# Attention scores from float32r halves on two 64-row halves of TensorE's array, in place of bf16 thirds on 96 rows

## The chip, the cores and the metric

The kernel runs on one core of one Trainium2 chip, in one launch. The metric is the device time in microseconds (us), the median of three runs: 1236.69 us, with 1232.07 and 1240.46 as the ends.

## What is computed

A transformer layer with float32 inputs and outputs: layer normalisation, causal attention from a latent, residual; layer normalisation, a top-2 mixture of 8 experts, residual. Cut to what matters here:

```python
# x: (4, 1024, 256), 16 heads of 16
c_kv = xn @ W_DKV                      # latent of 64
k = (c_kv @ W_UK).reshape(b, t, h, hd)
v = (c_kv @ W_UV).reshape(b, t, h, hd)
q = (xn @ W_UQ).reshape(b, t, h, hd)
scores = einsum('bqhd,bkhd->bhqk', q, k) / sqrt(hd)
scores = where(causal, scores, -inf)
probs = softmax(scores, axis=-1)
ctx = einsum('bhqk,bkhd->bqhd', probs, v).reshape(b, t, d)
x = x + ctx @ W_O
# then x = x + top-2 mixture of 8 experts of layernorm(x): W1 (256 -> 2 x 512, gated), W2 (512 -> 256)
```

## The kernel before

The program has four stages, one after the other, each ended by all engines: projection, attention, routing and experts.

*Projection* takes 4096 tokens in 8 chunks of 512. TensorE transposes the normalised tokens and makes the latent, q, k and v with float32 matmuls. q and k must keep float32 accuracy in bf16 matmuls, so each is split into three bf16 parts whose sum is the value: ScalarE copies the PSUM result to bf16 (L203), VectorE subtracts that from the PSUM result (`rest`, L266), ScalarE copies the rest to bf16 (L208), and GpSimd subtracts again for the third part (L183). SP then stores the parts of q and k (L144) and v (L147) in HBM.

*Attention* takes 64 pairs of batch and head in 16 quads of four heads. For a quad SP loads stacks `q_st` and `k_st` of 96 rows: six runs of 16 rows, in each one part of q against one part of k (`RUNS`), so that one contraction over 96 rows gives the score. A second set of three rows holds the row maxima, also in three bf16 parts, against rows of ones in `k_st`, so that a contraction over 99 rows gives score minus maximum. Four stacks (`RING`) are in use.

A quad has 12 units, each a block of 128 queries (or keys) by up to 512 columns, for the four heads. There are two passes over the scores. The maximum pass makes scores with queries as rows (`max_scores`, L666) in three PSUM banks (`NM`); VectorE reduces each block to its maximum, with the causal mask on diagonal blocks (L596, L599). After the 12 units VectorE combines the halves and splits the maxima in five small steps (`combine`, L568 to L583), TensorE transposes them (L714), ScalarE copies them to SBUF (L622), and SP copies them into the stack (L515). The probability pass makes scores with keys as rows (`prob_scores`, L684) in three other banks (`NS`), ScalarE takes the exponential (L640), GpSimd clears the triangle of diagonal blocks (L554), and TensorE multiplies with v (`products`, L703), the four heads side by side in strips of 32 columns, plain float32.

The order on TensorE is written out by hand. The probability pass runs 16 units (`LEAD`) behind the maximum pass and the products 2 units (`LAG`) behind the probabilities; within a unit, a maximum matmul and a probability matmul alternate, and the four products' matmuls come behind the four pairs:

```python
for unit in range(TOTAL + LEAD + LAG):
    if turned_at(unit) is not None:
        max_rows_transposed(turned_at(unit))
    for n in range(unit * QUAD, (unit + 1) * QUAD):
        if unit < TOTAL:
            max_scores(n)
        if 0 <= unit - LEAD < TOTAL:
            prob_scores(n - LEAD * QUAD)
    if unit - LEAD - LAG >= 0:
        products(unit - LEAD - LAG)
```

Each matmul waits until its bank is free: `max_scores` for VectorE (`bank_free`), `prob_scores` for ScalarE (`prob_ok`, three blocks back). `prob_scores` of a quad's first block also waits until the maximum rows have landed (`rows_in`). While attention runs, SP loads w1 (8 slices of 1 MB) and `FC_EARLY` = 3 slices of w2 for the experts, one per quad; the fourth slice of w2 is loaded in the routing stage (L917), between the loads of the next batch and the store of x2 (L923). VectorE's residual addition for the next batch (L1031) waits for that store.

*Routing* projects the context, adds the residual, normalises, picks experts and scatters rows by expert, batch by batch. *Experts* runs 71 tiles of 128 rows through W1 and W2 in plain float32 matmuls, one of which is recorded as two instructions.

## Time and profile before

| | |
|---|---|
| median of 3 runs | 1236.69 us (1232.07 to 1240.46) |
| span of the profiled execution | 1240.9 us |
| TensorE busy | 1069.9 us, 86% of the span |
| VectorE | 787.0 us, 63% |
| ScalarE | 491.9 us, 40% |
| GpSimd | 390.4 us, 31% |
| DMA | 121.22 MB, mean 98 GB/s |

The time to compare with is the median; durations of single instructions come from the profiled execution, whose span is given beside it. In the rows below PE is TensorE, PEld its weight loads, DVE VectorE, ACT ScalarE, POOL GpSimd and SP SyncE; L666 is line 666 of the kernel. Times are in us, unless a column says ns.

### The profile page before, as it was taken

To read this page: it belongs to the slowest core of one execution; us is meant where nothing else is said; L and a number is where in the kernel's file an instruction comes from. 1 tells how busy PE (TensorE), PEld (TensorE's weight loads), DVE (VectorE), ACT (ScalarE), POOL (GpSimd) and SP (SyncE) were. 2 spreads that over 40 slices of the span, in tenths; PEclk is the share of its full clock that TensorE was granted. 3 is DMA by queue.
4 is the path that set the end of the run, shared out by engine and by line. 5 is a ranking of instruction groups with operands and counts; after the bars stand their busy time and mean duration, and the time that the engine had idled before them with its cause. 6 is when DMAs were issued, how large, how long until landed. Compare 5 with 4: busy or idle time off the path is not lost. (4 is left out here: it accounts for less than half of the span.)

```text
span 1240.9 us, 19607 instructions
## 1 busy us (share of the span) xinstructions
PE 1069.9 (86%) x5364; PEld 554.3 (45%) x5365; DVE 787.0 (63%) x2352; ACT 491.9 (40%) x1043; POOL 390.4 (31%) x721
## 2 busy tenths in 40 slices
PE   6897599999999999998587553089999999999995
PEld 2443123333333333332176543046666666666663
DVE  5654599999999999894057443245555555555553
ACT  2333047777777777777501212012122122122121
POOL 2224513333333333333403235512222222222222
PEclk9878569999999999999987565589999999999998
DMA  2665974444466644400266641212232232232232
GB/s 91 208 189 188 199 157 104 122 113 113 116 141 135 132 82 79 80 20 30 66 220 193 225 124 68 103 39 44 46 50 42 45 49 42 44 49 42 44 49 25
DMA packets 102396, 121.22 MB, mean 98 GB/s; under 512 B 26352, under 2 KB 81776, under 8 KB 102320
## 3 DMA queue, kind: packets, MB, share of 16 engines
q1 hardware_dynamic: 89024, 102.55, 32.5%
q0 software_dynamic: 13296, 17.77, 8.6%
q8 instruction: 34, 0.56, 0.2%
q14 instruction: 42, 0.34, 0.1%
HBM read 70.27 MB, written 49.63 MB: 97 GB/s over the span
## 5 line engine op out<-in xcount | busy, mean ns | idle before, releaser
L640 ACT ACTIVATE b_prob<-b_prob_ps 128x512 f32<-128x512 f32 (+3 forms) x768 | 318.0, 506 | 103.2 <-PE b_prob_ps L684 101.2
L596 DVE CUSTOM_DVE_ANT_0 b_max_ps<-b_max_ps,b_mask_max 128x384 f32<-128x384 f32 (+3 forms) x512 | 246.7, 503 | 50.4 <-PE b_max_ps L666 47.9
L666 PE MATMUL b_max_ps<-b_k_st,b_q_st 96*128 96x512 bf16 (+3 forms) x768 | 253.5, 345 | 24.2 <-DMA b_k_st<-k_parts 21.8
L684 PE MATMUL b_prob_ps<-b_q_st,b_k_st 99*128 99x512 bf16 (+3 forms) x768 | 239.5, 330 | 10.5 <-ACT b_prob L640 6.6
L554 POOL TENSOR_SCALAR_AFFINE_SELECT b_prob<-b_prob 128x128 f32<-128x128 f32 x512 | 146.6, 292 | 308.6 <-ACT b_prob L640 300.9
L1352 POOL DMA_INDIRECT out_dram<-e_y,e_token x71 | 110.1, 1551 | 326.1 <-DVE e_y L1406 310.4
L599 DVE TENSOR_REDUCE b_neg_max<-b_max_ps 128x1 f32<-128x512 f32 x256 | 176.1, 688 | 5.1 <-PE b_max_ps L666 2.6
L666 PEld LDWEIGHTS b_max_ps<-b_k_st,b_q_st 96*128 96x128 bf16 x768 | 74.4, 99 | 202.0 <-DVE b_neg_max L596 110.1
L703 PE MATMUL b_acc_ps<-b_prob,b_v_aug 128*32 128x512 f32 (+3 forms) x1536 | 163.4, 498 | 0.2 <-POOL b_prob L554 0.2
L1459 PE MATMUL e_g_ps<-w_sb,e_rowsT 128*128 x284 | 135.5, 600 | 0.3 <-issue 0.3
L1459 PE MATMUL e_a_ps<-w_sb,e_rowsT 128*128 x284 | 134.0, 594 | 0.0
L684 PEld LDWEIGHTS b_prob_ps<-b_q_st,b_k_st 99*128 99x128 bf16 x768 | 74.1, 98 | 92.9 <-ACT b_prob L640 60.7
L1424 ACT ACTIVATE e_gate<-e_g_sum 128x512 f32<-128x512 f32 x71 | 44.7, 629 | 164.1 <-DVE e_g_sum L1386 164.1
L1429 ACT ACTIVATE e_hiddenT<-e_hiddenT_ps 128x512 f32<-128x512 f32 x71 | 42.4, 597 | 168.2 <-PE e_hiddenT_ps L1467 168.2
L1476 PE MATMUL e_y_ps<-w_sb,e_hiddenT 128*128 x426 | 103.7, 379 | 1.8 <-ACT e_hiddenT L1429 1.8
L1386 DVE TENSOR_TENSOR e_g_sum<-e_g_ps,m_b 128x512 f32<-128x512 f32 x71 | 49.1, 692 | 83.5 <-PE e_g_ps L1459 83.5
L1476 PEld LDWEIGHTS e_y_ps<-w_sb,e_hiddenT 128*128 128x128 f32 x426 | 80.8, 190 | 42.6 <-issue 35.2
L1389 DVE TENSOR_TENSOR e_hidden<-e_a_ps,m_b 128x512 f32<-128x512 f32 x71 | 49.1, 692 | 70.6 <-PE e_a_ps L1459 70.6
L1459 PEld LDWEIGHTS e_a_ps<-w_sb,e_rowsT 128*128 128x128 f32 x284 | 54.4, 191 | 68.8 <-issue 68.8
L596 DVE DVE_READ_ACCUMULATOR2_ANT b_neg_max<- 128x1 f32 x512 | 72.3, 141 | 0.0
L1459 PEld LDWEIGHTS e_g_ps<-w_sb,e_rowsT 128*128 128x128 f32 x284 | 48.9, 192 | 35.2 <-issue 35.2
L974 POOL DMA_INDIRECT slot_rows<-c_first_row,r_slot x32 | 31.7, 991 | 104.2 <-DVE r_slot L1108 95.6
(164 smaller groups left out, 1093.4 us busy)
## 6 DMA issues: line engine op xcount, KB each, us to landing
w_sb<-in_L_ffn_W SPq DMA_DIRECT2D x11, 1024.0 KB, 11.3
e_rows<-slot_rows SPq DMA_DIRECT2D x72, 129.0 KB, 2.1
ctx_cols<-b_ctx_out SPq DMA_DIRECT2D x16, 512.0 KB
q_parts<-a_part_q SPq DMA_DIRECT2D x8, 768.0 KB, 3.8
k_parts<-a_part_k SPq DMA_DIRECT2D x8, 768.0 KB, 4.2
b_q_st<-q_parts SPq DMA_DIRECT2D x16, 384.0 KB, 5.0
b_k_st<-k_parts SPq DMA_DIRECT2D x16, 384.0 KB, 7.7
a_x<-in_L_attn_x SPq DMA_DIRECT2D x8, 512.0 KB, 6.5
```

What stands on the lines that cost most here:

```text
L554: nc.gpsimd.affine_select(out=prob[n % NP][:, 0:P], in_=prob[n % NP][:, 0:P], compare_op=ALU.is_ge, fill=0.0, base=0, pattern=[[1, P]], ch ...
L596: nc.vector.tensor_tensor_reduce(scores, scores, mask_max[:, HALF - width:HALF], -1.0, -MASKED, ALU.add, ALU.min, to).then_inc(max_done, 1)
L599: nc.vector.tensor_reduce(to, scores, AX.X, ALU.max, negate=True).then_inc(max_done, 1)
L640: nc.scalar.activation(prob[n % NP][:, 0:width], prob_ps[n % NS][:, 0:width], ACT.Exp, scale=SCALE).then_inc(prob_ok, 1)
L666: nc.tensor.matmul(out[:, 0:width], q_st[g % RING][0:STACK, h, i * P:(i + 1) * P], k_st[g % RING][0:STACK, h, half * HALF:half * HALF + wi ...
L684: nc.tensor.matmul(prob_ps[n % NS][:, 0:width], k_st[g % RING][0:MAXROWS, h, j * P:(j + 1) * P], q_st[g % RING][0:MAXROWS, h, q0:q0 + widt ...
L703: mm = nc.tensor.matmul(acc_ps[half][32 * h:32 * h + 2 * HD, first:first + width], v_aug[g % 2][:, j, h, :, :].rearrange("p r s -> p (r s) ...
L1352: nc.gpsimd.indirect_dma_start(out=out, out_offset=bass.IndirectOffsetOnAxis(ap=token[c % B][:], axis=0), in_=y[c % B][:], in_offset=None, ...
L1386: nc.vector.tensor_tensor(g_sum[c % 2][:], g_ps[c % 2][:], bias_of(expert, 0, FF, FF), ALU.add).then_inc(g_sum_ok, 1)
L1389: nc.vector.tensor_tensor(hidden[c % 2][:], a_ps[c % 2][:], bias_of(expert, 0, 0, FF), ALU.add).then_inc(a_sum_ok, 1)
L1459: last = nc.tensor.matmul(out_ps[:], rowsT[c % 2][:, d * P:(d + 1) * P], w1_sb[:, bass.ds(expert, 1), d, first:first + FF].rearrange("p e ...
L1476: last = nc.tensor.matmul(y_ps[c % 2][:], hiddenT[c % 2][:, f * P:(f + 1) * P], w2_sb[f][:, bass.ds(expert, 1), :].rearrange("p e n -> p ( ...
```

## The change

q and k are split into two parts only, of type float32r: ScalarE's first copy and VectorE's subtraction write them (L203, L266), and the second copy and GpSimd's subtraction are gone. A score is now a contraction over three runs of 16 rows, 48 in all (`Q_RUNS` against `K_RUNS`). The parts take 4 bytes, so a stack has the same number of bytes: two heads beside each other on partitions 0 and 64, and two of such pairs in the free dimension. Even heads thus lie on the first 64 rows of the array and odd heads on the other 64. The probability pass takes its heads in swapped pairs (`prob_at`, h ^ 1), so that in the order on TensorE each maximum matmul and the probability matmul behind it lie on different halves. The maxima have two parts, three combine steps instead of five, and four row copies for a quad instead of three; the rows of ones in `k_st` are written by eight transfers in front of the second load instead of GpSimd's memsets; a load has eight transfers instead of six. Only two slices of w2 are loaded in attention (`FC_EARLY` = 2), and two in routing. Its core:

```diff
-FC_EARLY = 3
-PARTS = 3
-RUNS = [(0, 0, 3), (3 * HD, 0, 2), (5 * HD, 0, 1)]
-STACK = 6 * HD
+FC_EARLY = 2
+PARTS = 2
+ROW_TILE = 64
+STACK = 3 * HD
+Q_RUNS = [(0, 0, 1), (HD, 0, 2)]
+K_RUNS = [(0, 0, 2), (2 * HD, 0, 1)]
...
-                    sp.wait_ge(part3_ok[s], n + 1)
+                    sp.wait_ge(rest_ok[s], n + 2)
...
-            def second(n, c, s):
-                act.wait_ge(rest_ok[s], n + 2)
-                nc.scalar.activation(part[s][c][:, :, 1, :], rest[s][c][:], ACT.Copy).then_inc(part2_ok[s], 1)
...
-                nc.vector.tensor_tensor(rest[s][c][:], qk_ps[s][:], part[s][c][:, :, (0, 2)[s], :],
+                nc.vector.tensor_tensor(part[s][c][:, :, 1, :], qk_ps[s][:], part[s][c][:, :, 0, :].bitcast(F32),
...
+def prob_at(k):
+    unit, h = block_at(k)
+    return unit, h ^ 1
+def prob_index(unit, h):
+    return unit // 2 * 2 * QUAD + 2 * (h ^ 1) + unit % 2
+def last_index(unit):
+    return unit // 2 * 2 * QUAD + 2 * (QUAD - 1) + unit % 2
+def halves_of(h):
+    return h % 2 * ROW_TILE, h // 2
...
-        q_st = several(sb, RING, "b_q_st", [P, QUAD, SEQ], BF16)
-        k_st = several(sb, RING, "b_k_st", [P, QUAD, SEQ], BF16)
+        q_st = several(sb, RING, "b_q_st", [P, QUAD // 2, SEQ], F32R)
+        k_st = several(sb, RING, "b_k_st", [P, QUAD // 2, SEQ], F32R)
...
+            for w in range(RING):
+                for s in range(2):
+                    to = s * ROW_TILE + STACK
+                    sp.dma_start(k_st[w][to:to + PARTS, :, :].bitcast(F32).rearrange("o j (t n) -> o (j t) n", n=HALF),
+                                 ones_row[:].unsqueeze(1).to_broadcast([PARTS, QUAD, HALF])).then_inc(ones_in, 16)
...
+                at, j = halves_of(h)
+                nc.tensor.matmul(out[:, 0:width], q_st[g % RING][at:at + STACK, j, i * P:(i + 1) * P],
+                                 k_st[g % RING][at:at + STACK, j, half * HALF:half * HALF + width],
+                                 start=True, stop=True).then_inc(max_sc_ok, 1)
...
+                at, pair = halves_of(h)
+                nc.tensor.matmul(prob_ps[n % NS][:, 0:width],
+                                 k_st[g % RING][at:at + MAXROWS, pair, j * P:(j + 1) * P],
+                                 q_st[g % RING][at:at + MAXROWS, pair, q0:q0 + width], start=True,
+                                 stop=True).then_inc(prob_sc_ok, 1)
```

## Rows read from the trace of the kernel before

**Rows 1.** Busy time by stage: engine busy (instructions), granted clock, DMA share, GB/s.

```profile
126.40:170.70 44.30, 30.97 (x68) 7.18 (x69) 32.16 (x113) 1.55 (x2) 18.04 (x11) 0.50 0.92 179
170.70:574.30 403.60, 399.45 (x2816) 144.71 (x2813) 368.95 (x1244) 305.27 (x747) 142.74 (x482) 1.00 0.47 103
574.30:608.70 34.40, 27.58 (x191) 7.53 (x191) 0.91 (x5) 27.09 (x68) 12.35 (x44) 1.00 0.05 17
```

**Rows 2.** Order of time on SP's queue: the row copies of two successive quads.

```profile
358.36 1.80 SPq L515 DMA_DIRECT2D b_q_st<-b_max_rows  x3
...
385.77 1.80 SPq L515 DMA_DIRECT2D b_q_st<-b_max_rows  x3
```

**Rows 3.** Order of time on TensorE, about one unit: start, duration, instruction.

```profile
359.22 0.22 PE L684 MATMUL b_prob_ps<-b_q_st,b_k_st 99*128 99x128 bf16 x1
359.37 1.06 PE L703 MATMUL b_acc_ps<-b_prob,b_v_aug 128*32 128x512 f32 x8
360.37 0.28 PE L666 MATMUL b_max_ps<-b_k_st,b_q_st 96*128 96x256 bf16 x1
360.49 0.38 PE L684 MATMUL b_prob_ps<-b_q_st,b_k_st 99*128 99x512 bf16 x1
360.71 0.38 PE L666 MATMUL b_max_ps<-b_k_st,b_q_st 96*128 96x512 bf16 x1
...
361.72 0.64 PE L703 MATMUL b_acc_ps<-b_prob,b_v_aug 128*32 128x256 f32 x8
```

**Rows 4.** Order of time on VectorE: first block, and first combine step of quad 0.

```profile
138.22 0.57 DVE L596 CUSTOM_DVE_ANT_0 b_max_ps<-b_max_ps,b_mask_max 128x384 f32<-128x384 f32 x1 [20.61 <-PE b_max_ps L666]
...
162.10 0.17 DVE L568 TENSOR_TENSOR b_neg_max<-b_neg_max 128x16 f32<-128x16 f32 x1
```

**Rows 5.** Order of time in one unit of the tail, ScalarE and TensorE.

```profile
589.55 0.71 PE L684 MATMUL b_prob_ps<-b_q_st,b_k_st 99*128 99x512 bf16 x3
589.98 1.64 ACT L640 ACTIVATE b_prob<-b_prob_ps 128x512 f32<-128x512 f32 x4 [0.65 <-PE b_prob_ps L684]
590.63 0.28 PE L684 MATMUL b_prob_ps<-b_q_st,b_k_st 99*128 99x256 bf16 x1 [0.36 <-ACT b_prob L640]
590.85 0.85 PE L703 MATMUL b_acc_ps<-b_prob,b_v_aug 128*32 128x384 f32 x8
591.63 0.66 PE L684 MATMUL b_prob_ps<-b_q_st,b_k_st 99*128 99x512 bf16 x3
```

**Rows 6.** Busy time, twelve units of the tail; columns as in the first group.

```profile
582.12:608.10 25.98, 20.95 (x146) 5.72 (x145) 0.00 (x0) 20.43 (x51) 9.15 (x33) 1.00 0.06 22
```

**Rows 7.** Experts: one row of the chain of waits, in order of time.

```profile
836.49 1.73 PE e_y_ps L1476 x8
```

**Rows 8.** Weight loads, groups by line: busy us, mean ns, idle time before them.

```profile
L1476 PEld LDWEIGHTS e_y_ps<-w_sb,e_hiddenT 128*128 128x128 f32 x426 | 80.8, 190 | 42.6 <-issue 35.2
L1467 PEld LDWEIGHTS e_hiddenT_ps<-m_ident,e_hidden 128*128 128x128 f32 x284 | 35.5, 141 | 7.6 <-issue 0.5
L684 PEld LDWEIGHTS b_prob_ps<-b_q_st,b_k_st 99*128 99x128 bf16 x628 | 61.2, 97 | 61.0 <-ACT b_prob L640 35.1 <-DMA b_q_st<-b_max_rows 1.6
```

**Rows 9.** Order of time in projection; last, DMA issues with us to landing.

```profile
83.11 1.00 DVE L243 TENSOR_SCALAR a_var_eps<-a_mv 128x4 f32<-128x4 f32 x1
116.39 1.22 DVE L279 COPY a_v<-a_tv 128x1024 f32<-128x1024 f32 x1
120.89 0.62 SPq L147 DMA_DIRECT2D v_rows<-a_v  x1
k_parts<-a_part_k SPq DMA_DIRECT2D x8, 768.0 KB, 4.2
```

**Rows 10.** Routing: order of time, and busy time of 645 to 650 us.

```profile
640.97 0.43 SPq L923 DMA_DIRECT2D out_dram<-c_x  x1
645.00:650.00 5.00, 5.00 (x24) 4.38 (x24) 2.39 (x8) 0.00 (x0) 0.00 (x0) 0.99 1.04 379
651.28 2.48 DVE L1031 TENSOR_TENSOR c_x<-c_proj_ps,c_x_in 128x512 f32<-128x512 f32 x4 [3.89 <-PE c_proj_ps L1202]
```

More of the change, by code:

```diff
@@ L13 @@
 F32 = mybir.dt.float32
+F32R = mybir.dt.float32r
 BF16 = mybir.dt.bfloat16
@@ L83, in project_phase @@
         ckvT = sb("a_ckvT", [LAT, CHUNK])
-        part = [pair(sb, f"a_part_{qk}", [P, DC, PARTS, CHUNK], BF16) for qk in "qk"]
-        rest = [pair(sb, f"a_rest_{qk}", [P, DC, CHUNK]) for qk in "qk"]
+        part = [pair(sb, f"a_part_{qk}", [P, DC, PARTS, CHUNK], F32R) for qk in "qk"]
         v_out = pair(sb, "a_v", [P, TPC, D])
@@ L177, in _ @@
                     w_order_ok, 1)
-            def step(n, c, left):
-                for s in range(2):
-                    pool.wait_ge(part2_ok[s], n + 1)
-                    nc.gpsimd.tensor_tensor(part[s][c][:, :, (2, 0)[s], :], rest[s][c][:], part[s][c][:, :, 1, :],
-                                            ALU.subtract).then_inc(part3_ok[s], 1)
-            steps(pool, step)
         @block.scalar
@@ L216, in step @@
                 first(n, c, 1)
-                second(n, c, 0)
-                second(n, c, 1)
             take_root(0)
@@ L394, in attention_phase @@
     LEAD = UNITS + 4
-    COMBINE_STEPS = 5
+    COMBINE_STEPS = 3
     TURN = 2
@@ L480, in load @@
                 c, first = divmod(w * QUAD, P // HD)
-                for stack, parts, reverse in ((q_st[w], dram["q_parts"], False), (k_st[w], dram["k_parts"], True)):
-                    rows = parts[c].rearrange("g (r h) n -> (g r) h n", r=HD)
-                    for to, part, n in RUNS:
-                        start = (PARTS - n if reverse else part) * HD
-                        sp.dma_start(stack[to:to + n * HD, :, :],
-                                     rows[start:start + n * HD, first:first + QUAD, b * SEQ:(b + 1) * SEQ]).then_inc(
-                            stack_ok[w], 16)
+                for stack, parts, runs in ((q_st[w], dram["q_parts"], Q_RUNS), (k_st[w], dram["k_parts"], K_RUNS)):
+                    rows = parts[c].rearrange("g (r j s) n -> s (g r) j n", r=HD, s=2)
+                    for s in range(2):
+                        for to, start, n in runs:
+                            to += s * ROW_TILE
+                            sp.dma_start(stack[to:to + n * HD, :, :].bitcast(F32),
+                                         rows[s][start:start + n * HD, first // 2:first // 2 + QUAD // 2,
+                                                 b * SEQ:(b + 1) * SEQ]).then_inc(stack_ok[w], 16)
                 if g >= 2:
@@ L502, in _ @@
             load(0)
+            sp.wait_ge(ones_row_ok, 1)
+            for w in range(RING):
+                for s in range(2):
+                    to = s * ROW_TILE + STACK
+                    sp.dma_start(k_st[w][to:to + PARTS, :, :].bitcast(F32).rearrange("o j (t n) -> o (j t) n", n=HALF),
+                                 ones_row[:].unsqueeze(1).to_broadcast([PARTS, QUAD, HALF])).then_inc(ones_in, 16)
             for g in range(NQUAD + 2):
@@ L665, in max_scores @@
                 out = max_ps[place[item] % NM]
-                nc.tensor.matmul(out[:, 0:width], q_st[g % RING][0:STACK, h, i * P:(i + 1) * P],
-                                 k_st[g % RING][0:STACK, h, half * HALF:half * HALF + width],
+                at, j = halves_of(h)
+                nc.tensor.matmul(out[:, 0:width], q_st[g % RING][at:at + STACK, j, i * P:(i + 1) * P],
+                                 k_st[g % RING][at:at + STACK, j, half * HALF:half * HALF + width],
                                  start=True, stop=True).then_inc(max_sc_ok, 1)
             def prob_scores(n):
-                unit, h = block_at(n)
+                unit, h = prob_at(n)
                 g, u = divmod(unit, UNITS)
                 j, half, first, width, _ = prob_unit(u)
-                if unit == 0 and h == 0:
-                    pe.wait_ge(ones_ok, RING + 2)
-                if u == 0 and h == 0:
-                    pe.wait_ge(rows_in[g % RING], 16 * PARTS * (g // RING + 1))
+                if n == 0:
+                    pe.wait_ge(ones_in, 32 * RING)
+                    pe.wait_ge(ones_ok, 2)
+                if n % PER_QUAD == 0:
+                    pe.wait_ge(rows_in[g % RING], 32 * PARTS * (g // RING + 1))
                 if n >= NS:
@@ L697, in products @@
                 if diagonal:
-                    cut = sum(prob_unit(block_at(n)[0])[4] for n in range(index_of(u, QUAD - 1) + 1))
+                    cut = sum(prob_unit(prob_at(n)[0])[4] for n in range(last_index(u) + 1))
                     pe.wait_ge(causal_ok, g * DIAGONALS + cut)
                 else:
-                    pe.wait_ge(prob_ok, index_of(unit, QUAD - 1) + 1)
+                    pe.wait_ge(prob_ok, last_index(unit) + 1)
                 for h in range(QUAD):
```

84 lines of the change are left out of this document (41 added, 43 removed).

## The prediction

> **What bounds the kernel now.** I read first the busy time by stage [rows 1]. The attention stage is 403.6 us of steady work in which maximum and probability matmuls share TensorE, preceded by 44.3 us in which VectorE alone sets the pace (TensorE at 0.50 of its clock, its lower level of 1.2 GHz) and followed by 34.4 us without maximum matmuls. In the steady part TensorE is busy 399.45 of 403.60 us, VectorE 368.95, ScalarE 305.27. A busy TensorE says little by itself, so the second view is a single quad of heads: the row copies on SP's queue start at 358.36 and again at 385.77, 27.41 us apart [rows 2], and 14.7 such quads fill the 403.6 us.
>
> What does TensorE do in 27.41 us? From the order of time [rows 3]: a matmul of 512 columns is followed by the next 0.22 us later (360.49 to 360.71), one of 256 after 0.12 (360.37 to 360.49); by the same slope 384 columns take about 0.165 and 128 about 0.06. Both score streams have, per quad, 24 blocks of 512 and 8 each of 384, 256 and 128 columns: 24 x 0.217 + 8 x (0.165 + 0.115 + 0.06) = 7.9 us, twice 15.8 us. The products of a 512-wide unit hold the array from 359.37 to 360.37, 1.00 us; over the widths of the twelve units (six of 512, two each of 384, 256 and 128, at about 0.79, 0.57 and 0.36) that is 9.4 us. The step from a 128-column score matmul to the products takes 0.15 us (359.22 to 359.37) instead of 0.06: 0.1 us lost, twelve times. The sum is 26.4 us of 27.41. So the array's own time is the bound today, almost exactly.
>
> VectorE's floor comes from the stretch in which it never rests: its first quad goes from 138.22 to 162.10, 23.9 us [rows 4], with the combine steps 24.3. ScalarE: four blocks in 1.64 us [rows 5], some 19 us per quad.
>
> Now the stage that decides what overlapped scores can bring: the tail, where TensorE has only probability scores and products, half the score work. It needs 25.98 us for twelve units [rows 6]. The rows of one unit tell why [rows 5]: three score matmuls start at 589.55, ScalarE starts on the first at 589.98, and the fourth must wait for a PSUM bank until 590.63; then its own 0.22 us, then the products of 384 columns until 591.63. The cycle is 0.43 (matmul to reader) + 0.65 (reader back to the bank) + 0.22 + 0.78 = 2.08 us, with no array time of a maximum matmul in it. It is a loop through three banks, cut once per unit by the products. The change leaves three banks, four heads and the products as they are.
>
> **The change part by part.** (1) *Scores on two halves.* If two neighbours in the queue run beside each other, the 15.8 us fall to 7.9 and array time to 18.5 us per quad. Then the bank loop of the tail is the bound: 25.98 us. No row shows a float32r matmul or 64-row tiles; for the rate the near ends are bf16 (0.22 us for 512 columns) and one of the two instructions into which a plain float32 matmul is recorded: eight of 256 columns in 1.73 us, 0.216 each, twice the 0.115 of bf16 [rows 7]. I take the bf16 rate: the plain float32 matmul pays for splitting its operands, and here the kernel has split them itself, into the three products of halves that its 48 rows hold.
>
> (2) *Weight loads.* Today's loads of 128 bf16 columns last 97 ns, a float32 transposition's 128 columns 141 and a plain float32 load 190 [rows 8]. I take 141, the lowest with four-byte weights: 0.043 us more than now. Where a matmul waits for a bank I let its load wait too, so this adds to the loop twice in each unit, after the products and at the fourth bank: 2 x 0.043 = 0.09 us. Bounds: 0 (loads pulled ahead) and 2 x 0.093. The pace is then 25.98/12 + 0.09 = 2.25 us, 27.0 us per quad against 27.41: -0.4 x 14.7 = -6.0 us. In the tail the same 0.09 us costs 18 x 0.09 = +1.6.
> The Trainium skill, "TensorE: Matmul & The Clock Gate", section on weight-path perf modes, speaks against the change: fast weight load needs 128 weights and an input type other than FP32. The trace agrees as far as it goes, in the 97 and the 190 ns of [rows 8]. The same skill, "TensorEngine Tiling (Array Packing)", PSUM Bottleneck, says that tiling speeds up TensorE but not the evacuation of PSUM; by this page the pace would be the loop's 25.98 to 27.0, as taken.
>
> (3) *Clock.* TensorE is at 1.00 (2.4 GHz) in the tail, though it streams only one score stream and the products; it was at 0.50 in the first stretch with maximum matmuls alone [rows 1, 6]. The overlapped main part is like the tail, so 1.00 is kept.
>
> (4) *Maximum rows.* Combine falls from five steps to three, each about 0.1 us of VectorE, hidden because VectorE has 3 us of room per quad. The transposition is of 128x128 float32, 0.05 us more. The row copies become four instead of three, at 0.6 us each on SP: with a landing about 1.8 us after its issue (as long as all three issues take together now, and less than half of the 4.2 us of a large transfer [rows 9]) the last is there at 358.36 + 3 x 0.6 + 1.8 = 361.96, where the first probability matmul of the quad now runs at about 362.3, behind the products that start at 361.72 (256 columns, 0.57) [rows 2, 3]. With shorter units that margin is near nothing: 0 to 0.3 us per quad, I take +1 in all. Without this margin each quad would pay the 0.6 us in full, 9 us.
>
> (5) *Projection.* ScalarE's second copy and GpSimd's subtraction go. TensorE waits for neither, but three of the eight small VectorE operations at L243, in front of the next chunk's normalisation, last 1.00 us [rows 9], where the like of them (L568, on more columns) takes 0.17 [rows 4]: 3 x 0.83 = -2.5 us, if GpSimd's subtraction is what holds them up (0 to -2.5). At the end the stores of q and k wait for GpSimd, and v is issued behind them at 120.89; attention begins at 126.4 [rows 1, 9]. Now v follows its own copy at 117.7 (after 116.39 + 1.22), 3.2 us earlier, but q and k carry 1 MB each, not 768 KB. Such a transfer lands 4.2 us after its issue [rows 9]; a third more is 1.4 us, and as both are ahead of v it may come twice. I take -2.2 (-3.2 to +1).
>
> (6) *Entry into attention.* The first load is eight transfers instead of six, of the same bytes; VectorE's first block waits for it until 138.22 [rows 4], 11.8 us after the stage's start. Two more issues at 0.6 us [rows 2] are 1.2 us, mostly beside the transfers under way: I take +0.4 (-2 if rows of twice the bytes move faster, to +1.5). The eight small fills of ones stand ahead of load 1 on SP, 8 x 0.6 = 4.8 us; load 1 is needed when the second quad starts, at about 162 [rows 4], twice the first load's 11.8 us after the first block, so they are covered. If they were not, quad 1 would wait those 4.8 us. GpSimd's memsets of the ones are needed only by the first probability matmul, at 170.7 [rows 1]; taking them away is worth nothing.
>
> (7) *One slice of w2 later.* The routing stage loads 2 MB of w2, not 1, ahead of the store at 640.97; the DMA engines are full (1.04) at 379 GB/s in 645 to 650, and VectorE's addition for the next batch (L1031, 651.28) needs that store [rows 10]. 1 MB/379 GB/s = +2.8 us (0, since TensorE is named as what ended that wait, to +4).
>
> Sum: -6.0 + 1.6 + 1 - 2.5 - 2.2 + 0.4 + 2.8 = -4.9 us on an execution with a span of 1240.9 us; nothing is shown around the span, which is 0.3% above the median of 1236.69. On the median: **1231.8 us**.
>
> **The rivals.** *A, the loop opens (0.27).* The time from matmul to reader (0.43) contains the way through 99 rows; half an array may be quicker, and loads for one half may run under the other's matmul. For it: the loads are short against a 512-column matmul. Against it: nothing in the tail is shortened by overlap as such. The pace lies between 25.98 and VectorE's 24.3; at 25.98 main gives -21 and at 25.5 -28, others -1: 1215 to 1208. The rule of "TensorEngine Tiling (Array Packing)", Overview, in the Trainium skill promises up to twice the speed for contractions of at most 64 rows; no row here shows two matmuls on row halves, and by it the array's share would fall as in (1).
>
> *B, slower: loads on the loop (0.20).* If a float32r load costs what a plain float32 load does, 190 ns, the loop gets 2 x 0.093 = 0.19 us: 2.35 us a unit, 28.2 per quad. That is +0.8 x 14.7 = +11.6, tail +3.3, others -0.5: 1251 us. It decides against the change from an addition of about 0.12 us per unit on ((27.41 - 25.98)/12). For it: the wait at the fourth bank (590.63). Halves that do not overlap at all, with single-pass loads, come to much the same, 26.4 + some exposed loads.
>
> *C, a slow format or a lower clock (0.10).* If float32r streams 512 columns in 0.43 us, twice bf16, overlap only pays for that; the loop has 0.22 more in two places: 2.6 us, 31 per quad, +53: some 1288 us. At half clock it is the same order or more. Against it is (1) and (3).
>
> *D, the two halves never run side by side, and loads stay hidden (part of the forecast's 0.43).* Then the array's 26.4 stands and main is unchanged: 1238 us.
>
> **How the numbers follow.** Forecast with D 0.43, A 0.27, B 0.20, C 0.10. Within 1% (12.4 us, about what a measurement of this kernel can tell from no change) lie nearly all of the forecast and four tenths of B: 0.47. Faster by over 1%: A and a little of the forecast, 0.30. Slower: the rest of B, and C, 0.23. The range takes in A's 1208 and B's 1251 with the small terms' bounds, leaving out C and an edge of A: 1207 to 1252.
>
> **What would show it.** Right: row copies 26.8 to 27.3 us apart; two matmuls whose starts are far less than 0.2 us apart, one of them 512 wide; loads of 141 ns; TensorE waiting for ScalarE and VectorE rather than busy; the tail 36 us; attention beginning at 121 to 122; L1031 of the second batch 2 to 3 us later after its stage begins. Wrong: starts still 0.22 us apart in the steady part (no overlap), loads of 190 ns (B), a clock under 1.00 in attention, or a wait for the row copies in each quad. The forecast is most exposed in (2): 0.09 us per unit is nearly all of the distance between a clear gain and none.

## The result, and the profile after

The changed kernel takes 1346.47 us (median of 4 runs, 1315.83 to 1365.93), the kernel before 1234.4 on the same chip: ratio 1.069 (1.061 to 1.077). The ratio goes by the two faster of the four, since the others lie over 3% above the fastest, and the profile is of the slowest. The forecast was 1231.8, its range 1207 to 1252: even the fastest lies far outside, on the slow side. The executions differ more than those of any other kernel here, and go with their mean granted clock, which in the profiled one rises and falls within attention: 1365.93 us at 0.78, 1364.22 at 0.784, 1328.73 at 0.818, 1315.83 at 0.832.

The profiled execution spans 1364.2 us. Busy time by stage (columns as in [rows 1]), from the first load of attention on: entry, maximum alone, main, tail, routing.

```profile
111.10:122.50 11.40, 0.00 (x0) 0.03 (x1) 0.48 (x1) 0.00 (x0) 3.47 (x7) 0.50 1.00 167
122.50:156.40 33.90, 33.19 (x67) 17.71 (x67) 32.73 (x111) 1.55 (x2) 0.64 (x1) 0.50 0.90 175
156.40:684.40 528.00, 521.91 (x2804) 244.98 (x2804) 369.28 (x1212) 309.29 (x743) 142.39 (x481) 0.67 0.36 77
684.40:740.40 56.00, 48.06 (x221) 16.36 (x219) 2.12 (x9) 29.45 (x72) 13.05 (x46) 0.57 0.03 11
740.40:932.80 192.40, 87.12 (x456) 80.65 (x456) 86.70 (x317) 28.00 (x36) 70.35 (x84) 0.65 0.51 166
```

Against [rows 1], the main stage has grown from 403 to 528 us and the tail from 37.4 (cut at the same events) to 56.0; the granted clock, 1.00 in both before, is 0.67 and 0.57. VectorE and ScalarE are as busy as before (369 and 309 us). Here is each of this study's kernels, cut at the same events: first load of attention, first maximum matmul, first probability matmul, last maximum matmul, last product, first matmul of the experts. Lengths in us, granted clock in brackets (the traces have no record of the clock in the first 17 us, and the views count them as full).

| kernel | projection | entry | maximum alone | main | tail | routing | experts | us per quad at its commonest clock |
|---|---|---|---|---|---|---|---|---|
| before | 126.4 (.85) | 11.3 | 32.4 (.50) | 402.8 (1.00) | 37.4 (1.00) | 198.5 | 432.1 | 27.4 (1.00) |
| after | 111.1 (.97) | 11.4 | 33.9 (.50) | 528.1 (.67) | 56.0 (.57) | 192.5 | 431.3 | 28.4 (1.00), 42.1 (.50) |
| one half | 119.4 | 11.1 | 34.6 | 641.2 (.51) | 59.6 (.50) | 191.5 | 431.7 | 44.6 (.50) |
| bf16 halves | 109.0 (.98) | 6.6 | 32.3 | 402.9 (.93) | 51.6 (.55) | 193.4 | 431.6 | 27.4 (.94), 26.3 (1.00) |
| maximum twice | 115.6 | 11.1 | 41.7 | 464.9 (.95) | 58.1 (.52) | 191.5 | 431.6 | 30.8 (1.00) |
| no third part | 116.0 (.93) | 11.2 | 32.4 | 402.9 (.99) | 37.4 (1.00) | 192.2 | 432.2 | 27.4 (1.00) |
| w2 as after | 126.2 (.85) | 11.5 | 32.4 | 402.7 (.99) | 37.4 (1.00) | 196.8 | 432.7 | 27.4 (1.00) |
| 48 rows, before | 142.5 | 7.5 | 32.4 | 721.9 (.50) | 53.0 (.50) | 197.9 | 431.2 | 49.6 (.50) |
| zeros to 64 rows | 152.0 | 11.1 | 33.8 | 420.6 (.98) | 53.6 (.62) | 197.3 | 432.5 | 28.4 (1.00) |
| all rows | 151.7 | 17.9 | 34.0 | 433.9 (1.00) | 40.0 (1.00) | 190.4 | 432.4 | 29.6 (1.00) |
| zeros, later | 115.4 | 16.4 | 43.7 | 420.9 (.98) | 49.4 (.72) | 192.3 | 431.7 | 28.4 (1.00) |
| bf16, zeros | 113.3 | 9.6 | 32.9 | 387.6 (.98) | 52.2 (.53) | 194.5 | 431.8 | 26.3 (1.00) |
| bf16, zeros, tail kept | 109.7 | 9.6 | 32.8 | 387.3 (.98) | 37.7 (1.00) | 195.5 | 431.8 | 26.3 (1.00) |
| third part on VectorE | 145.4 (.80) | 11.7 | 32.4 | 402.5 (.99) | 37.4 (1.00) | 188.1 | 431.8 | 27.4 (1.00) |

(Where zeros or ones are written before the first load, that time is in the projection's column.) From before to after: projection -15.3, entry and maximum alone +1.6, main +125.3, tail +18.6, routing -6.0, experts -0.8: +123.4.

The row copies on SP's queue, as in [rows 2]: two quads at full clock, and two at half.

```profile
230.16 2.46 SPq L525 DMA_DIRECT2D b_q_st<-b_max_rows  x4
258.59 2.43 SPq L525 DMA_DIRECT2D b_q_st<-b_max_rows  x4
295.77 2.42 SPq L525 DMA_DIRECT2D b_q_st<-b_max_rows  x4
337.83 2.43 SPq L525 DMA_DIRECT2D b_q_st<-b_max_rows  x4
```

28.43 us and 42.06 us. Busy time in a stretch at each clock:

```profile
229.00:268.00 39.00, 37.85 (x272) 17.46 (x264) 34.02 (x112) 28.31 (x72) 14.52 (x50) 1.00 0.40 91
272.00:410.00 138.00, 138.00 (x638) 65.15 (x637) 84.28 (x273) 71.28 (x169) 32.16 (x108) 0.50 0.43 95
```

In the second TensorE is recorded busy for 138.00 of 138.00 us, and still gets half its clock; before, in twelve units of the tail, it was busy 20.95 of 25.98 us at 1.00 [rows 6]. So recorded busy time isn't what the clock follows. (The Trainium skill, "TensorE: Matmul & The Clock Gate", section "What's actually happening", says that a hardware block sets the clock by how busy the engine has been. Taken as the busy time of a profile, these rows contradict it.)

Do the halves overlap? In order of time on TensorE, first at full clock, then at half; the counterpart is [rows 3].

```profile
245.29 1.06 PE L716 MATMUL b_acc_ps<-b_prob,b_v_aug 128*32 128x512 f32 x8
246.28 0.38 PE L676 MATMUL b_max_ps<-b_k_st,b_q_st 48*128 48x256 f32 x1
246.29 0.49 PE L696 MATMUL b_prob_ps<-b_q_st,b_k_st 50*128 50x512 f32 x1
246.50 0.39 PE L676 MATMUL b_max_ps<-b_k_st,b_q_st 48*128 48x512 f32 x1
246.62 0.22 PE L696 MATMUL b_prob_ps<-b_q_st,b_k_st 50*128 50x128 f32 x1
246.68 0.33 PE L676 MATMUL b_max_ps<-b_k_st,b_q_st 48*128 48x256 f32 x1
246.74 0.39 PE L696 MATMUL b_prob_ps<-b_q_st,b_k_st 50*128 50x512 f32 x1
247.25 0.49 PE L676 MATMUL b_max_ps<-b_k_st,b_q_st 48*128 48x512 f32 x1
...
302.01 0.47 PE L676 MATMUL b_max_ps<-b_k_st,b_q_st 48*128 48x128 f32 x1
302.01 0.79 PE L696 MATMUL b_prob_ps<-b_q_st,b_k_st 50*128 50x512 f32 x1
302.28 0.73 PE L676 MATMUL b_max_ps<-b_k_st,b_q_st 48*128 48x512 f32 x1
...
304.11 1.93 PE L716 MATMUL b_acc_ps<-b_prob,b_v_aug 128*32 128x512 f32 x8
```

They do: a matmul of 512 columns starts 0.01 us after its neighbour (246.29), where [rows 3] had 0.22 between starts. At full clock the fourth pair starts 0.51 us after the one before (246.74 to 247.25). What it waits for stands in front of its weight load:

```profile
247.25 0.18 PEld L676 LDWEIGHTS b_max_ps<-b_k_st,b_q_st 48*128 48x128 f32 x1 [0.44 <-DVE b_neg_max L605]
```

It is a bank of the maximum, which VectorE has to read first. The wait of [rows 5] is another: a bank of the probabilities, and ScalarE. At half clock the eight products take 1.93 us instead of 1.06. Weight loads by group, at full clock and at half (columns as in [rows 8]):

```profile
L676 PEld LDWEIGHTS b_max_ps<-b_k_st,b_q_st 48*128 48x128 f32 x67 | 11.1, 184 | 16.0 <-DVE b_neg_max L605 10.7 <-DVE b_neg_max L608 3.4 <-issue 0.6
L676 PEld LDWEIGHTS b_max_ps<-b_k_st,b_q_st 48*128 48x128 f32 x157 | 44.0, 311 | 54.7 <-issue 28.4 <-DVE b_neg_max L605 14.5 <-DVE b_neg_max L608 11.8
```

A float32r load is 184 ns at full clock, near the 190 of a plain float32 one in [rows 8]. The projection, in order of time, and then its busy time in the changed kernel and in the one before:

```profile
86.33 0.17 DVE L227 TENSOR_SCALAR a_var_eps<-a_mv 128x4 f32<-128x4 f32 x1
103.91 1.21 DVE L263 COPY a_v<-a_tv 128x1024 f32<-128x1024 f32 x1
105.15 0.37 SPq L147 DMA_DIRECT2D v_rows<-a_v  x1
```

```profile
20.00:100.00 80.00, 71.83 (x226) 34.71 (x225) 52.99 (x136) 22.82 (x28) 0.00 (x0) 1.00 0.76 262
```

```profile
20.00:110.00 90.00, 83.92 (x222) 39.66 (x221) 55.90 (x136) 36.30 (x41) 28.13 (x14) 0.83 0.54 169
```

L227 is L243 of before, now always 0.17 us; v's store follows its copy by 1.24 us (4.50 in [rows 9]); and the clock is 1.00 where it was 0.83.

### The profile page after: what moved, and what is told of

The parts are those of the page before. It is cut to its first block and busy times, and to the rows that moved or that the text cites. A ratio compares the mean times of both kernels' runs of the same rounds, so it can differ in the third digit from the quotient of the medians.

```text
span 1364.2 us, 19581 instructions
## 1 busy us (share of the span) xinstructions
PE 1190.9 (87%) x5364; PEld 660.2 (48%) x5365; DVE 786.3 (58%) x2321; ACT 482.6 (35%) x1027; POOL 343.0 (25%) x702
## 5 line engine op out<-in xcount | busy, mean ns | idle before, releaser
L676 PE MATMUL b_max_ps<-b_k_st,b_q_st 48*128 48x512 f32 (+3 forms) x768 | 325.0, 538 | 25.9 <-DMA b_k_st<-k_parts 19.1
L696 PE MATMUL b_prob_ps<-b_q_st,b_k_st 50*128 50x512 f32 (+3 forms) x768 | 326.0, 523 | 7.9 <-ACT b_prob L649 7.9
L676 PEld LDWEIGHTS b_max_ps<-b_k_st,b_q_st 48*128 48x128 f32 x768 | 180.8, 260 | 251.9 <-issue 95.0
L716 PE MATMUL b_acc_ps<-b_prob,b_v_aug 128*32 128x512 f32 (+3 forms) x1536 | 239.8, 711 | 0.0
L696 PEld LDWEIGHTS b_prob_ps<-b_q_st,b_k_st 50*128 50x128 f32 x768 | 164.4, 256 | 51.7 <-ACT b_prob L649 36.2
L1489 PE MATMUL e_y_ps<-w_sb,e_hiddenT 128*128 x284 | 73.1, 380 | 1.8 <-ACT e_hiddenT L1442 1.8
L1489 PE MATMUL e_y_ps<-m_w,e_hiddenT 128*128 x284 | 72.9, 379 | 0.0
L1489 PEld LDWEIGHTS e_y_ps<-w_sb,e_hiddenT 128*128 128x128 f32 x284 | 53.8, 190 | 38.9 <-issue 35.2
```

The lines of the kernel that those rows point to most:

```text
L676: nc.tensor.matmul(out[:, 0:width], q_st[g % RING][at:at + STACK, j, i * P:(i + 1) * P], k_st[g % RING][at:at + STACK, j, half * HALF:half ...
L696: nc.tensor.matmul(prob_ps[n % NS][:, 0:width], k_st[g % RING][at:at + MAXROWS, pair, j * P:(j + 1) * P], q_st[g % RING][at:at + MAXROWS, ...
L716: mm = nc.tensor.matmul(acc_ps[half][32 * h:32 * h + 2 * HD, first:first + width], v_aug[g % 2][:, j, h, :, :].rearrange("p r s -> p (r s) ...
L1489: last = nc.tensor.matmul(y_ps[c % 2][:], hiddenT[c % 2][:, f * P:(f + 1) * P], w2_sb[f][:, bass.ds(expert, 1), :].rearrange("p e n -> p ( ...
```

## The experiments

Each ratio is against the kernel before on the same chip, with its 95% interval. The expectations of runs 1, 2, 3 and 8 were written before those of the others, and a theory's number means in each what that text says.

**1. Both matmuls of a pair in the same half.**

```diff
 def prob_at(k):
-    return unit, h ^ 1
+    return unit, h
```

> The changed kernel, but the probability pass takes its heads in plain order, so that a maximum matmul and the probability matmul behind it lie on the same 64 rows and four matmuls in a row share a half. Theory 1 (the halves side by side leave the array idle between bank waits, and the granted clock falls): the clock is 1.00 in the main part of attention, quads take 28 to 29 us at the weight loads of 180 ns, and the whole takes 1215 to 1240 us. Theory 2 (the long float32r weight loads alone are the loss): quads no better than the 28.4 us that the changed kernel shows at clock 1.00, same total as theory 1. Theory 3 (float32r itself is what lowers the clock, however the halves are used): the clock stays at 0.5 to 0.8, 1310 us or more.

1491.47 us (1472.87 to 1493.64), ratio 1.200 (1.191 to 1.209). Main, then tail (columns as above):

```profile
165.10:806.30 641.20, 640.81 (x2803) 310.45 (x2804) 381.88 (x1208) 318.87 (x742) 142.39 (x481) 0.51 0.29 63
806.30:865.90 59.60, 51.89 (x223) 17.51 (x220) 2.21 (x9) 29.90 (x72) 13.05 (x46) 0.50 0.03 10
```

Neighbours one after the other don't bring the clock back: it is 0.51, lower still, so theory 1 is out. Lying side by side isn't what costs the clock; it rather helps to keep it. Theory 3, the format, stays open until runs 2, 4 and 6.

**2. The halves in bf16.** The parts, stacks, row tiles and maximum rows are bf16 instead of float32r (the remainder of q and k is rounded to bf16; no third part); lay-out, rows and pairs as in the changed kernel.

```diff
-        q_st = several(sb, RING, "b_q_st", [P, QUAD // 2, SEQ], F32R)
+        q_st = several(sb, RING, "b_q_st", [P, QUAD // 2, SEQ], BF16)
```

> The changed kernel with both parts of q, k and the maxima as bf16 instead of float32r (the scores keep about 16 bits instead of 24): weight loads fall back to about 98 ns, halves stay side by side. Theory 1: the clock still falls, quads between 26.5 us (where it is 1.00) and over 38 us (where it is 0.50), 1290 to 1350 us. Theory 2: quads 26 to 27 us throughout and about 1195 us. Theory 3: clock 1.00, the same 1195 us.

1229.78 us (1224.93 to 1240.85, 10 runs), ratio 0.996 (0.993 to 0.999).

```profile
147.90:550.80 402.90, 384.33 (x2804) 109.75 (x2803) 355.57 (x1212) 302.38 (x743) 142.56 (x481) 0.93 0.27 75
550.80:602.40 51.60, 43.48 (x219) 8.19 (x219) 2.06 (x9) 28.96 (x72) 13.07 (x46) 0.55 0.03 11
```

All three totals are missed, and the time is that of the kernel before within 1%. The clock is 0.93 in main, but 0.55 in the tail, where only probability matmuls of 50 rows and the products are left. The format has a large part in main, and yet cannot be all of it.

**3. Each maximum matmul twice.** Nothing is read from the first of the two.

```diff
-                nc.tensor.matmul(out[:, 0:width], ...).then_inc(max_sc_ok, 1)
+                for _ in range(2):
+                    mm = nc.tensor.matmul(out[:, 0:width], ...)
+                mm.then_inc(max_sc_ok, 1)
```

> The changed kernel with every maximum matmul issued twice into the same bank: 768 matmuls more, no other change. Theory 1: the added columns keep the clock at 1.00 for most of attention; quads 29 to 31 us there, 1250 to 1290 us, so faster than the changed kernel in spite of the added work. Theories 2 and 3: the added loads and columns cost 3 us or more per quad at an unchanged clock, 1370 us or more.

1305.22 us (1301.28 to 1316.22), ratio 1.053 (1.049 to 1.057).

```profile
300.00:500.00 200.00, 199.72 (x1567) 104.95 (x1567) 166.44 (x536) 138.92 (x333) 65.06 (x218) 1.00 0.45 99
```

768 matmuls more make the changed kernel faster, though the total is 15 us over theory 1's range: the ratio is 1.053 against 1.069, and the two intervals are only just apart. It holds 1.00 through nearly all of main (30.8 us per quad), and pays for the tail, which has no maximum matmuls to double (0.52). So the clock follows work in the array. What kind of work it counts, busy time (138.00 of 138.00 at 0.50) doesn't say; the next three runs ask for rows.

**4. The kernel before with 48 rows.** Of its three runs of rows only the first; bf16, no halves side by side, everything else as before. The scores lack the smaller parts of q and k.

```diff
-RUNS = [(0, 0, 3), (3 * HD, 0, 2), (5 * HD, 0, 1)]
-STACK = 6 * HD
+RUNS = [(0, 0, 3)]
+STACK = 3 * HD
```

> The kernel before, its scores cut to the first of its three runs of rows: 48 rows in the maximum matmuls (96 before), 51 in the probability matmuls (99), bf16, heads one after the other in the same rows; its results lack the smaller parts of q and k. Everything else, with GpSimd's third part, is as before. Theory 1 (the number of rows lowers the granted clock, whatever their format): main stage well under 1.00, tail near 0.5 as with the bf16 halves (0.55), tail 50 us or more instead of 37.4, total 15 to 120 us above before. Theory 2 (the four-byte format with its loads of 180 ns lowers the clock in the main stage; few rows count only in the tail): main 0.93 to 1.00 at 27.4 us per quad, tail 50 us, total 1240 to 1255. Theory 3 (rows do not count; the bf16 halves lost the clock in the tail because two matmuls are done in the time of one): main and tail 1.00, total 1230 to 1240.

1589.03 us (1587.2 to 1594.09), ratio 1.279 (1.270 to 1.288).

```profile
182.40:904.30 721.90, 721.90 (x2804) 207.84 (x2804) 408.34 (x1240) 357.37 (x744) 142.39 (x481) 0.50 0.17 44
```

Theory 1, and far beyond its figure. The same number of bf16 matmuls, of the same columns, with loads of the same number of columns (97 ns at full clock before, 135 at half here), costs 721.9 us instead of 402.8 once it fills 48 and 51 rows instead of 96 and 99, and TensorE is "busy" all the time. (16 us of the total are the wait for the ones, ahead of the first load.)

**5. The changed kernel with zeros up to 64 rows.** The 14 free rows of each half are zeros and are contracted too.

```diff
-STACK = 3 * HD
+STACK = ROW_TILE - PARTS
 MAXROWS = STACK + PARTS
...
+            for tile in q_st + k_st:
+                for to in (P // 4, P // 4 * 3):
+                    nc.vector.memset(tile[to:to + P // 4, :, :].bitcast(F32), 0.0).then_inc(pad_ok, 1)
```

> The changed kernel with the 14 free rows of each half filled with zeros and contracted too (62 rows in the maximum matmuls, 64 in the probability matmuls; the rows of the maximum lie at 62 and 63). Same results, same matmuls, loads and waits; at the start of the stage VectorE writes the zeros, which may add 5 to 10 us there. Theory 1 (rows in use are what the clock goes by, zeros or not): the clock in main rises well above 0.67, total under 1300. Theory 2 (only rows with changing data count, or rows do not count at all): clock in main 0.6 to 0.8 as in the changed kernel, total 1320 to 1370.

1300.68 us (1296.47 to 1302.68), ratio 1.045 (1.038 to 1.053).

```profile
196.90:617.50 420.60, 404.69 (x2806) 186.41 (x2805) 364.51 (x1212) 302.13 (x743) 143.37 (x481) 0.98 0.45 97
617.50:671.10 53.60, 45.47 (x220) 15.62 (x219) 2.07 (x9) 29.38 (x72) 13.15 (x46) 0.62 0.03 11
```

```profile
L701 PEld LDWEIGHTS b_prob_ps<-b_q_st,b_k_st 64*128 64x128 f32 x768 | 126.1, 194 | 54.5 <-ACT b_prob L654 41.4 <-issue 8.5 <-DMA b_q_st<-b_max_rows 1.8
```

The same matmuls with zeros added: main goes from 528.1 to 420.6 us, the clock from 0.67 to 0.98. The total, 1300.68, is at the edge of theory 1's "under 1300". The zeros cost some 40 us ahead of the stage, as VectorE writes them first, which hides part of the gain in the total. The last row, a group of weight loads, says that the wait for the row copies is 1.8 us in all sixteen quads.

**6. Both halves at once.** Each score matmul of run 5 contracted over 126 or 128 rows, one at a time. The heads of a pair are added and the exponential's scale is a 128th, so the results aren't attention's.

```diff
-                nc.tensor.matmul(out[:, 0:width], q_st[g % RING][at:at + STACK, j, ...],
+                nc.tensor.matmul(out[:, 0:width], q_st[g % RING][0:ROW_TILE + STACK, j, ...],
```

> The same with each float32r score matmul contracted over 126 or 128 rows, both halves at once: the heads of a pair are added, the exponential has a 128th of its scale, so the results are not attention's; counts, widths, loads and waits are those of the changed kernel, but no two matmuls lie side by side. Theory 1 (rows): clock near 1.00 in main and tail, 28 to 30 us per quad at that clock, total 1240 to 1280, far below the 1491 of the run in which all heads share one half with 48 rows. Theory 2 (format): clock near 0.5, total about 1490 again.

1304.92 us (1301.95 to 1309.53), ratio 1.051 (1.044 to 1.058).

```profile
203.60:637.50 433.90, 432.99 (x2805) 255.52 (x2804) 374.37 (x1211) 305.34 (x744) 142.33 (x481) 1.00 0.43 94
637.50:677.40 39.90, 34.20 (x220) 14.14 (x218) 1.85 (x9) 28.43 (x72) 13.10 (x46) 1.00 0.04 15
```

float32r, no overlap, and 1.00 in main and tail: with all rows in use neither the format nor the order takes the clock away. At 48 and 50 rows in each half the format does count: the changed kernel's 0.67 against the 0.93 of run 2. With the 1491 us of run 1 beside it, rows are the difference. Here one matmul follows the other, so the rate of float32r can be read, 0.23 us for 512 columns:

```profile
332.46 0.40 PE L703 MATMUL b_prob_ps<-b_q_st,b_k_st 128*128 128x512 f32 x1
332.69 0.40 PE L683 MATMUL b_max_ps<-b_k_st,b_q_st 126*128 126x512 f32 x1
```

(The total lies 25 us over the range given: again the 40 us of zeros ahead, which I had left out.)

**7. The kernel before with one slice of w2 less loaded early.**

```diff
-FC_EARLY = 3
+FC_EARLY = 2
```

> The kernel before with only two slices of w2 loaded early instead of three, nothing else. As predicted for this part of the change: the routing stage 2.8 us longer (0 to 4), total +0.2%. Rival: other waits end last there, total within 0.1% of before. The routing stage of the changed kernel is 6 us shorter than that of before, which this edit alone should not give.

1241.11 us (1239.62 to 1246.93, 10 runs), ratio 0.999 (0.995 to 1.003). That interval has room for the +0.2% as well as for nothing, so the trace must tell. VectorE's addition for the second batch and for the third, the counterpart of [rows 10]:

```profile
653.73 2.48 DVE L1031 TENSOR_TENSOR c_x<-c_proj_ps,c_x_in 128x512 f32<-128x512 f32 x4 [8.51 <-DMA out_dram<-c_x]
675.93 1.29 DVE L1031 TENSOR_TENSOR c_x<-c_proj_ps,c_x_in 128x512 f32<-128x512 f32 x2
```

The forecast wait is there: with the last product of attention at 610.2 in both, the second batch's addition comes 2.5 us later than before (651.28), and now the store ends its wait. But it is made good within the batch: the third batch's comes at 675.93, before it was 676.54. So the rival has it for the stage (196.8 us instead of 198.5), with other waits ending last further on. Nor is the 6 us by which the changed kernel's routing is shorter an effect of the change: among these kernels the stage varies from 188 to 198 us, in ones that don't touch it.

**8. No third part.** The kernel before without GpSimd's subtraction; the third part of q and k is zeros, written once.

```diff
-                    nc.gpsimd.tensor_tensor(part[s][c][:, :, (2, 0)[s], :], rest[s][c][:], part[s][c][:, :, 1, :],
-                                            ALU.subtract).then_inc(part3_ok[s], 1)
...
+                    nc.gpsimd.memset(part[s][c][:, :, (2, 0)[s], :], 0.0).then_inc(part3_ok[s], 1)
```

> The kernel before, with the third bf16 part of q and k left out (GpSimd's subtraction is gone, a constant zero is stored in its place, so the scores keep about 16 bits). If GpSimd's subtraction is what held up the projection, that stage falls from 126 us to 111 to 115 us and TensorE's clock stays at 1.00 in it, 1222 us in all; if ScalarE's second copy is the cause, or the larger share of the change in how the parts are stored, it falls by 5 us at the most.

1225.13 us (1223.27 to 1228.62), ratio 0.989 (0.986 to 0.993); projection 116.0 instead of 126.4, its clock 0.93 instead of 0.85: 1 us above the range given and not quite the full clock, but far more than the rival's 5. In order of time, VectorE's small operation and GpSimd's fill:

```profile
11.99 3.00 DVE L239 TENSOR_SCALAR a_var_eps<-a_mv 128x4 f32<-128x4 f32 x1
...
52.32 0.17 DVE L239 TENSOR_SCALAR a_var_eps<-a_mv 128x4 f32<-128x4 f32 x1
```

```profile
11.34 1.83 POOL L182 MEMSET a_part_q<- 128x1024 bf16 x2
13.12 1.84 POOL L182 MEMSET a_part_k<- 128x1024 bf16 x2
```

The operation is slow only while GpSimd writes, here once, for 3.00 us of its four fills: that part of step (5) is shown.

**9. The third part on VectorE** instead of GpSimd, after the statistics.

```diff
+                for s in range(2):
+                    dve.wait_ge(part2_ok[s], n + 1)
+                    nc.vector.tensor_tensor(part[s][c][:, :, (2, 0)[s], :], rest[s][c][:], part[s][c][:, :, 1, :],
+                                            ALU.subtract).then_inc(part3_ok[s], 1)
```

> The kernel before with its third part of q and k written by VectorE instead of GpSimd, after the statistics; exact, attention unchanged. If GpSimd's subtraction slows the projection by its speed and by holding up VectorE (without it the stage took 116.0 instead of 126.4): 116 to 121, total 1227 to 1233. Rival (2.4 us more of VectorE per chunk are on the path): 126 or more, total at or above before.

1246.18 us (1242.68 to 1254.77, 9 runs), ratio 1.006 (1.003 to 1.009). A miss, the rival and more: projection 145.4 us at 0.80 (before, 0.85). VectorE is in front of TensorE in each chunk, and a TensorE that waits more also gets less clock.

**10. Zeros that arrive later.** Run 5 with the zeros brought by sixteen small transfers behind the first load.

```diff
+            for w in range(RING):
+                for stack in (q_st[w], k_st[w]):
+                    for to in (3 * HD, ROW_TILE + 3 * HD):
+                        sp.dma_start(stack[to:to + FILL, :, :]...,
+                                     zero_rows[:].unsqueeze(1).to_broadcast([FILL, QUAD, HALF])).then_inc(stack_ok[w], 16)
```

> The changed kernel with the 14 free rows of each half filled with zeros and contracted (62 and 64 rows), the zeros brought by sixteen small transfers behind the first load instead of by VectorE ahead of it. Same results. Theory 1 (the rows in use decide the clock): main at 0.98 or more and 28.4 us per quad, 418 to 422 us; projection 111, entry 12 to 15, tail 53.6 as in the run with zeros by VectorE: total 1260 (1255 to 1270), so the format's longer loads alone leave it 1.5 to 2% above before. Rival (the long pause ahead of that run's attention stage had a part in its clock): main under 0.9, total above 1300.

1274.48 us (1271.63 to 1278.32), ratio 1.031 (1.026 to 1.035), against the changed kernel's 1.069 (another chip, but the intervals lie far apart). Main is as expected (420.9, 0.98). The total is 4 us over its range: the fills stand ahead of load 1 on SP, which is issued only at 145.93, and the stretch of maximum matmuls alone grows by 10 us.

```profile
138.69 7.19 SPq L515 DMA_DIRECT2D b_k_st<-b_ones_row  x8
145.93 1.80 SPq L489 DMA_DIRECT2D b_q_st<-q_parts  x4
```

**11. The same zeros with the bf16 halves of run 2.**

```diff
-        zero_rows = sb("b_zero_rows", [FILL, HALF])
+        zero_rows = sb("b_zero_rows", [FILL, HALF], BF16)
```

> The same zeros with bf16 halves (two bf16 parts in 48 rows, weight loads of 96 ns instead of 180; the float32r remainder is rounded to bf16). Theory 1 with the loop of the tail: main at 1.00 and 26.0 to 26.4 us per quad, 385 to 390 us against 402.9 of the bf16 run without zeros; tail 50; total 1210 to 1218, the first version faster than before by over 1.5%. Rival (27.4 is the loop's own pace, its clock of 0.94 does no harm): main 402, total 1228 to 1232.

1217.85 us (1207.77 to 1223.75, 6 runs), ratio 0.982 (0.977 to 0.987).

```profile
155.80:543.40 387.60, 364.47 (x2803) 105.71 (x2803) 354.74 (x1210) 303.09 (x743) 142.64 (x481) 0.98 0.28 78
543.40:595.60 52.20, 44.17 (x220) 8.21 (x219) 2.08 (x9) 28.98 (x72) 13.06 (x46) 0.53 0.03 11
```

```profile
L684 PEld LDWEIGHTS b_max_ps<-b_k_st,b_q_st 62*128 62x128 bf16 x768 | 59.2, 95 | 242.9 <-DVE b_neg_max L613 164.0 <-DVE b_neg_max L616 55.8 <-issue 19.3
```

Total and main are as expected. 26.3 us per quad at 1.00 is near the tail's 25.98 [rows 6], but it isn't the tail's loop alone. In the row above, 219.8 of the 242.9 us for which the loads of the maximum matmuls stood back ended with VectorE; those of the probability matmuls ended with ScalarE for 56.3. And VectorE is busy for 240.28 of 260 us:

```profile
L704 PEld LDWEIGHTS b_prob_ps<-b_q_st,b_k_st 64*128 64x128 bf16 x768 | 57.1, 94 | 85.0 <-ACT b_prob L657 56.3 <-issue 13.4 <-DMA b_q_st<-b_max_rows 2.2
200.00:460.00 260.00, 245.48 (x1910) 70.96 (x1911) 240.28 (x821) 205.68 (x506) 96.83 (x327) 1.00 0.32 88
```

That is 24.3 us of VectorE per quad, its floor in the prediction, and the waits for two sets of three banks make the rest. Runs 10 and 11 have the same rows, pairs and clock, and differ in the format: 28.43 against 26.29 us per quad, 0.178 us per unit, while a load is 184 against 95 ns. Two loads per unit on the path would be 2 x 0.089 = 0.178: the figure fits, and the load of 247.25 above does wait for its bank, but that it is two in each unit wasn't tested apart.

**12. The tail kept busy.** Run 11 with a spare matmul beside each probability matmul of the last quad, in the other half, into a bank of the maximum that nobody reads any more.

```diff
+                if n >= (TOTAL - UNITS) * QUAD:
...
+                    at, pair = halves_of(h ^ 1)
+                    nc.tensor.matmul(max_ps[(h ^ 1) % 2][:, 0:width], q_st[g % RING][at:at + STACK, pair, ...],
+                                     k_st[g % RING][at:at + STACK, pair, q0:q0 + width], start=True, stop=True)
```

> The bf16 kernel with zeros, and in the last quad of the tail a spare matmul in the other half beside each probability matmul, as in the main stage, into a bank of the maximum that nobody reads any more. It adds 48 matmuls and takes nothing away. Theory 1 (the tail's clock falls for want of rows in use): tail 36 to 40 us at 0.8 to 1.00 instead of 50, total 1198 to 1208. Rival (a spare matmul is only more work): tail 50 us or longer, total at or above that of the run without it.

1209.68 us (1206.35 to 1213.79, 6 runs), ratio 0.978 (0.974 to 0.981). The same two stretches together (they are cut 3.8 us behind the last maximum matmul that is read; with the cut at that matmul, as in the table, the tail is 37.7 us, within theory 1's range):

```profile
152.20:543.40 391.20, 367.52 (x2827) 106.45 (x2828) 356.79 (x1218) 306.74 (x751) 144.76 (x485) 0.98 0.27 78
543.40:577.20 33.80, 26.73 (x249) 7.33 (x245) 0.00 (x0) 25.19 (x63) 12.11 (x43) 1.00 0.05 18
```

425.0 us against the 439.8 of run 11: 48 matmuls that nobody needs give back 14.8 us between the two profiles (of executions of 1223.75 and 1206.35 us). The medians differ by 8 us, 2 us short of theory 1's total, and the intervals of the two ratios overlap: the tail's clock and length are clear, the gain in the total isn't. This version beats both kernels, by 2.2% (1.9 to 2.6) the one before, but with q and k in two bf16 parts instead of three, so with less accurate scores.

## Why the prediction was wrong

**Step (3), the clock, failed.** It said "The overlapped main part is like the tail, so 1.00 is kept", and gave a lower clock a share of rival C's 0.10. I likened the stages by how much they stream. But the tail of before fills 99 rows, and the changed main part 48 and 50 of each half, for the time in which halves overlap. Runs 4 (rows taken from before: 1.00 to 0.50), 5 and 10 (zeros added: 0.67 to 0.98), 6 (all rows, no overlap: 1.00) and 12 (a half filled in the tail: back to 1.00) show that the granted clock goes by how many rows are contracted as well as by time, and that zeros count. Whether it is rows, cells or words streamed that count, they can't tell. Its price in the profiled execution: main 528.1 against 420.6 to 420.9 with the rows filled, 107 us; tail 15 to 16, by the 40.0 of run 6 and the 14.8 of run 12. Together that is all of the +123; the rest cancels. At the 1328.73 and 1315.83 us of two other executions, 37 and 50 less than the profiled one's, the price would be an estimated 86 and 73 us, if all of that difference is clock, as their mean clocks suggest. Rows and format act together here: with bf16's shorter loads the same 48 and 50 rows lose 15 us of main, not 107 (402.9 in run 2, 387.6 in run 11).

**Step (2), the weight loads, was right in mechanism, as far as shown, and wrong in size.** The load waits with its matmul for the bank (247.25 above), and runs 10 and 11 fit two of them on the path in each unit. I took 141 ns; it is 184, near the upper bound of 190. Rival B put the pace at 28.2 us per quad; at full clock it is 28.43, (28.43 - 27.41) x 14.7 = 15 us of the 18 by which main grows in runs 5 and 10 (402.8 to 420.6 and 420.9); the other 3 are in run 5 the first quad, not yet at full clock, and in run 10 largely one later quad, in which the clock was 0.50 for 10 us. What came is B together with the lower clock of C. With the clock's 107 + 16 us taken off, the profiled 1364.2 would be an estimated 1241, the time before: the loads' +18 and +3 paid for by the projection's -15 and a routing stage that happened to be 6 shorter.

**Step (1) held for the array, and only in part for the loop.** The halves run side by side (starts 0.01 us apart), float32r streams at nearly the bf16 rate (0.23 us for 512 columns in run 6, 0.22 in [rows 3]), and with bf16 loads and full clock waits for banks set the pace, 26.3 us per quad in run 11 against 25.98 forecast. But the step took over the tail's loop, which goes through ScalarE and has no maximum matmul in it. In main most of the waiting is for VectorE's reading of the maximum banks, and VectorE had only 2 us of room per quad; no run separates the two sets of banks, so that the figure comes so near is partly luck. Rival A, a loop that opens (25.98 or less), did not come, D is refuted by the starts.

**Step (4)** was of the right order: 1.8 us in run 5 where I took 1.0 for main. **Step (5)** gave -4.7, measured -15.3. The stalls are GpSimd's doing (run 8) and v's store follows its copy; k's transfers of 1 MB land 4.3 us after their issue, not 1.4 later than the smaller ones' 4.2. The remainder has no term in my sum: I left out that TensorE's clock in the projection, 0.83 in the middle (the row of before above), might change: over the whole stage it went from 0.85 to 0.97. Run 8, with GpSimd's subtraction gone, already has 10.4 of the 15.3; run 9 shows the other direction. That a rising clock is cause and not only companion of the shorter stage was not tested alone. **Step (6)**: +0.1 for +0.4; the eight fills of ones were covered, as said, but run 10 shows how near their cover was to its end. **Step (7)**: +2.8 forecast. The wait came as described, 2.5 us in run 7, but isn't on the path to the end of the stage: the third batch starts as early as before.

Slower by over 1% had 0.23. At half clock the array's own 18.5 us per quad are 37, already above the loop: a product that the rows would have given, and that the prediction put into one half-sentence of rival C.

## What to carry to other kernels

Whoever packs small contractions into half the rows should price TensorE at both of its clock levels, and look in the profile at the granted clock of the new stage before anything else; busy time doesn't show the loss. If rows are free, fill them with zeros and contract them: it costs no array time, and took 107 us off main between the profiled executions (the ratio of the whole went from 1.069 to 1.031, in run 10). Where a loop of waits is the bound, array time saved is worth only the distance to that loop, and a longer weight load on it takes that back.

## What the hardware showed that I had not expected

- The granted clock falls to 0.50 with TensorE recorded busy without a pause: 721.9 us at 48 and 51 rows, 402.8 us at 1.00 with 96 and 99. Rows of zeros count as use: 0.67 becomes 0.98.
- More matmuls can be faster: with 768 more the ratio went from 1.069 to 1.053; with 48 more in the tail, that stage from 52.2 to 37.7 us.
- A load of 128 columns of float32r weights takes 184 ns at full clock and about 311 at half, 48 rows deep, and the same 184 with 62; in bf16 95 ns, in halves as well.
- VectorE's operation on 4 columns, 0.17 us otherwise, took 3.00 us while GpSimd filled tiles.
